# The experts' matmuls of a fused attention and soft-MoE block in three passes over high and low parts

## The reference, cut to what matters

```python
x = layernorm(x) ; se = layernorm(slot_embeds) * scale            # B=4, E=16, S=64, D=256, F=512, DO=256
logits = einsum('bnd,esd->bnes', x, se)
slots = einsum('bnd,bnes->besd', x, softmax(logits, axis=1))
gate = gelu(einsum('besd,edf->besf', slots, Wg) + bg)             # per expert: 256 x 256 by 256 x 512
up = einsum('besd,edf->besf', slots, Wu) + bu                     # the same size
eout = einsum('besf,efo->beso', gate * up, Wd) + bd               # 256 x 512 by 512 x 256
out = x_in + attention(xn) + einsum('bns,bso->bno', combine, eout)
```

## Time and profile before

| | us |
|---|---|
| median of 3 runs (lowest, highest) | 2759.08 (2755.48, 2759.23) |
| the profiled execution's own time | 2755.84 |
| its span, first to last instruction | 2753.9 |
| TensorE busy in the span | 2589.1 (94%) |
| VectorE, ScalarE, GpSimd busy | 2078.8 (75%), 1634.3 (59%), 443.7 (16%) |
| experts' stage, first matmul to first matmul of combine | 2273.5 to 2445.15 |

### The profile page before, as it was taken

One profiled execution on the slowest core, in us unless ns is written; L12 is line 12 of the kernel. 1 busy time (PEld: TensorE's weight loads), 2 busy tenths in 40 slices (PEclk: granted clock), 3 DMA queues, 4 the chain that ended last, 5 costly groups with the idle time before them and its releaser, 6 DMA issues. The chain is left out here.

```text
span 2753.9 us, 47808 instructions
## 1 busy us (share of the span) xinstructions
PE 2589.1 (94%) x16291; PEld 1543.9 (56%) x16291; DVE 2078.8 (75%) x5010; ACT 1634.3 (59%) x3370; POOL 443.7 (16%) x611
## 2 busy tenths in 40 slices
PE   7866999999999999999999999989999999999999
PEld 4433444444444444444444444347878788889999
DVE  8966989899899889989988998738474522346665
ACT  4531777777777777777777777866364522122221
POOL 4533111111111111111111111124121100100000
PEclk9975999999999999999999999999999999999999
DMA  7983362133033123303303000025343345435554
GB/s 244 315 241 40 46 84 34 17 46 45 6 48 45 22 30 46 39 12 46 46 14 40 8 6 8 8 104 214 106 170 136 109 161 180 163 132 194 193 189 156
DMA packets 177641, 257.63 MB, mean 94 GB/s; under 512 B 48756, under 2 KB 126712, under 8 KB 175896
## 3 DMA queue, kind: packets, MB, share of 16 engines
q1 hardware_dynamic: 160824, 239.26, 34.2%
q10 hardware_dynamic: 16608, 15.73, 1.9%
HBM read 158.30 MB, written 95.45 MB: 92 GB/s over the span
## 5 line engine op out<-in xcount | busy, mean ns | idle before, releaser
L768 ACT ACTIVATE att_pr<-att_ring 128x512 f32<-128x512 f32 (+3 forms) x2560 | 1174.4, 548 | 398.7 <-PE att_ring L848 391.4
L815 DVE TENSOR_REDUCE att_mx<-att_ring 128x1 f32<-128x512 f32 x1536 | 968.0, 680 | 77.0 <-PE att_ring L861 73.9
L861 PE MATMUL att_ring<-att_ks,att_qs 48*128 48x512 f32 (+3 forms) x1920 | 647.7, 422 | 17.0 <-ACT att_pr L768 7.0
L848 PE MATMUL att_ring<-att_qs,att_ks 64*128 64x512 f32 (+3 forms) x1920 | 575.0, 406 | 9.8 <-DMA att_qs<-att_mrow 4.9
L848 PEld LDWEIGHTS att_ring<-att_qs,att_ks 64*128 64x128 f32 x1920 | 300.5, 186 | 406.2 <-DVE att_mx L815 143.4
L821 DVE CUSTOM_DVE_ANT_0 att_junk<-att_ring,w_causal 128x256 bf16<-128x256 f32 (+3 forms) x1024 | 466.0, 486 | 67.6 <-PE att_ring L861 42.2
L887 PE MATMUL att_acc<-att_pr,att_v 128*32 128x512 f32 (+3 forms) x3840 | 451.5, 542 | 2.7 <-ACT att_cT L779 1.5
L861 PEld LDWEIGHTS att_ring<-att_ks,att_qs 48*128 48x128 f32 x1920 | 307.4, 185 | 144.7 <-ACT att_pr L768 106.4
L726 POOL TENSOR_SCALAR_AFFINE_SELECT att_pr<-att_pr 128x512 f32<-128x512 f32 x256 | 163.1, 637 | 1049.5 <-ACT att_pr L768 1049.5
L861 PE MATMUL att_ring<-g_ks,g_qs 48*128 48x512 f32 (+3 forms) x640 | 225.5, 463 | 17.2 <-PEq L137 7.8
L1452 ACT CAST com_e1h<-com_tp 128x1024 fp32r<-128x1024 f32 x64 | 64.8, 1017 | 236.4 <-PE com_tp L1512 236.4
(11 more groups left out here) (162 smaller groups left out, 3225.1 us busy)
## 6 DMA issues: line engine op xcount, KB each, us to landing
slot_exps<-dis_e SPq DMA_DIRECT2D x64, 512.0 KB, 2.7
com_e<-slot_exps SPq DMA_DIRECT2D x64, 512.0 KB, 3.5
att_qs<-q_parts SPq DMA_DIRECT2D x72, 256.0 KB, 12.0
q_parts<-proj_part SPq DMA_DIRECT2D x32, 512.0 KB, 4.3
dis_y<-y_rows SPq DMA_DIRECT2D x32, 512.0 KB, 3.9
att_ks<-k_parts SPq DMA_DIRECT2D x72, 128.0 KB, 12.8
y_rows<-proj_y SPq DMA_DIRECT2D x16, 512.0 KB, 4.4
y_cols<-proj_yT SPq DMA_DIRECT2D x16, 512.0 KB, 5.3
```

Source lines behind the costliest of these rows:

```text
L768: nc.scalar.activation(pr[:, s % NPR, h, off:CH], spot(("s", s, h)), ACT.Exp, scale=float(HD) ** -0.5).then_inc(exp_done, 1)
L815: nc.vector.tensor_reduce(dst, spot(e), AX.X, ALU.max).then_inc(mb_used, 1)
L848: nc.tensor.matmul(spot(e), ks[g][r, kb * P:(kb + 1) * P], qs[g][r, c, hf * CH + off:(hf + 1) * CH], start=True, stop=True).then_inc(sT_re ...
L861: nc.tensor.matmul(spot(e), qs[g][r, c, q0:q0 + P], ks[g][r, j * CH:j * CH + wd], start=True, stop=True).then_inc(mb_ready, 1)
```

## The change: what it does

Expert 0's gate and up products stay as they are. For all others, and for all sixteen down products, both operands are held as a high part (rounded to fp32r) and a low part (the difference), and each matmul becomes three: high x high, high x low, low x high. The splits are made beside the matmuls:

- ScalarE makes the high parts of Wg, Wu and Wd (`gate_high`, `up_high`, `down_high`, 128 x 1024 each) and of the four pieces of h (`hidden_high`).
- VectorE makes the low parts of Wu and Wd (`up_low`, `down_low`) and of h (`hidden_low`). Its output step for an expert now comes one expert later: `output(e - 2)` in round e.
- GpSimd makes both parts of the slots (`slots_parts`) and the low part of Wg (`gate_low`), and the low parts of pairs as before.
- The raw weights' rings have two buffers in place of four. `load(e)` waits for the splits of expert e - 2; `load_bias` is as it was, and stands between one `load` and the next.

```diff
-    NB = 4
+    NR, NB = 2, 4
...
-        wg, wu = a.sb("wg", [P, NB, DK, F]), a.sb("wu", [P, NB, DK, F])
-        wd = a.sb("wd", [P, NB, FB, D])
+        wg, wu, wd = a.sb("wg", [P, NR, DK, F]), a.sb("wu", [P, NR, DK, F]), a.sb("wd", [P, NR, FB, D])
...
             def _(sp):
+                def load(e):
+                    if e < E:
+                        for dst, src, loaded, split, n in ((wg, "Wg", gate_in, wg_split, e - NR),
+                                                           (wu, "Wu", up_in, wu_split, e - NR),
+                                                           (wd, "Wd", down_in, wd_split, e - NR + 1)):
+                            if e >= NPRE + NR:
+                                sp.wait_ge(split, n)
+                            sp.dma_start(dst[:, e % NR], io[src][e]).then_inc(loaded[e % NR], 16)
...
                 for e in range(E):
                     if e >= NPRE:
-                        load_gu(e + NB)
-                    if e + NB < E:
-                        load_bias(e + NB)
-                    if e >= NPRE:
-                        load_down(e + NB)
+                        load(e + NR)
+                    load_bias(e + NB)
                     if e == E - NB:
                         com["load_first"](sp)
...
             def _(act):
+                def gate_high(e):
+                    wait_weights(act, e, gate_in)
+                    if e >= 3:
+                        act.wait_ge(gu_ready, 2 * (e - 2) + 2)
+                    nc.scalar.copy(wgh[:, e % 2], weights(e)[0]).then_inc(wg_high, 1)
...
+                gate_high(1)
+                up_high(1)
+                down_high(0)
                 for e in range(E):
-                    for f in range(FB):
...
+                    gelus(e, (0, 1))
+                    if 1 <= e < E - 1:
+                        gate_high(e + 1)
+                    hidden_high(e, (0, 1))
+                    if 1 <= e < E - 1:
+                        up_high(e + 1)
+                    gelus(e, (2, 3))
+                    if e >= 1:
+                        down_high(e)
+                    hidden_high(e, (2, 3))
                     if e >= 3 and e % 2:
                         round_pair((e - 3) // 2)
...
             def _(dve):
+                def up_low(e):
+                    dve.wait_ge(wu_high, e)
+                    nc.vector.tensor_tensor(wul[:, e % 2], weights(e)[1], wuh[:, e % 2].bitcast(F32),
+                                            ALU.subtract).then_inc(wu_split, 1)
...
-                hidden(0)
-                for e in range(1, E):
-                    hidden(e)
-                    output(e - 1)
-                output(E - 1)
+                for e in range(E):
+                    hidden(e, (0, 1))
+                    if e >= 2:
+                        output(e - 2)
+                    hidden_low(e, (0, 1))
+                    if 1 <= e < E - 1:
+                        up_low(e + 1)
+                    hidden(e, (2, 3))
+                    if e >= 1:
+                        down_low(e)
+                    hidden_low(e, (2, 3))
...
             def _(pool):
+                for e in range(1, E):
+                    slots_parts(e)
+                    gate_low(e)
+                    if e >= 5 and e % 2:
+                        pair_low((e - 5) // 2)
...
                 def gate_up(e):
-                        pe.wait_ge(gu_in[q], 16 * 2 * ((e - NPRE) // NB + 1))
+                        pe.wait_ge(sl_split, e)
+                        pe.wait_ge(wg_split, e)
+                        pe.wait_ge(wu_split, e)
...
+                                    for lhs, rhs in ((hi, slh), (hi, sll), (lo, slh)):
+                                        last = nc.tensor.matmul(dst[:, f, :], lhs[:, e % 2, k, cols], rhs[:, e % 2, k, :],
+                                                                start=(k == 0 and rhs is slh and lhs is hi),
+                                                                stop=(k == DK - 1 and lhs is lo))
...
                 def down(e):
+                    pe.wait_ge(wd_split, e + 1)
+                    pe.wait_ge(hl_ready, FB * e + FB)
```

More of the change, by code:

```diff
@@ L1327, in _, with slots_parts, gate_low, pair_low @@
             def _(pool):
-                for s in range(SB - 1):
+                def slots_parts(e):
+                    src = pre["slots"][:, :, e // 2, e % 2]
+                    part = lambda t: t[:, e % 2].rearrange("p k (b j) -> p b k j", b=B)
+                    if e == 1:
+                        pool.wait_ge(pre["slots_in"], 16 * (B - 1))
+                    if e >= 3:
+                        pool.wait_ge(gu_ready, 2 * (e - 2) + 2)
+                    nc.gpsimd.tensor_copy(part(slh), src).then_inc(sl_high, 1)
+                    pool.wait_ge(sl_high, e)
+                    nc.gpsimd.tensor_tensor(part(sll), src, part(slh).bitcast(F32), ALU.subtract).then_inc(sl_split, 1)
+                    pool.wait_ge(sl_split, e)
+                def gate_low(e):
+                    pool.wait_ge(wg_high, e)
+                    nc.gpsimd.tensor_tensor(wgl[:, e % 2], weights(e)[0], wgh[:, e % 2].bitcast(F32),
+                                            ALU.subtract).then_inc(wg_split, 1)
+                    pool.wait_ge(wg_split, e)
+                def pair_low(s):
                     pool.wait_ge(high_ready, s + 1)
@@ L1331, in _ @@
                                             ALU.subtract).then_inc(low_ready, 1)
+                    pool.wait_ge(low_ready, s + 1)
+                for e in range(1, E):
[3 more added lines that the diff above has]
+                        pair_low((e - 5) // 2)
+                pair_low(SB - 2)
             @block.tensor
@@ L1361, in down @@
                     for r in range(RB):
+                        rows = slice(r * P, (r + 1) * P)
                         for f in range(FB):
-                            last = nc.tensor.matmul(op[:, e % 2, r, :], h[:, e % 2, f, r * P:(r + 1) * P],
-                                                    weights(e)[2][:, f, :], start=(f == 0), stop=(f == FB - 1))
+                            for lhs, rhs in ((hh, wdh), (hh, wdl), (hl, wdh)):
+                                last = nc.tensor.matmul(op[:, e % 2, r, :], lhs[:, e % 2, f, rows], rhs[:, e % 2, f, :],
+                                                        start=(f == 0 and lhs is hh and rhs is wdh),
+                                                        stop=(f == FB - 1 and lhs is hl))
                     last.then_inc(o_ready, 1)
```

124 lines of the change are left out of this document (77 added, 47 removed).

## The result

| | before | changed |
|---|---|---|
| median, us (lowest, highest; 4 runs each) | 2758.45 (2755.48, 2759.23) | 2890.3 (2889.12, 2891.83) |
| the profiled execution | 2755.84 | 2889.38 |
| first gelu of the experts' stage | 2278.82 | 2277.85 |
| first matmul of the combine stage | 2445.15 | 2578.39 |

The changed kernel is slower: ratio 1.0486, 95% interval [1.0473, 1.0499]. The forecast was 2856 with a range of 2822 to 2882, so the direction was right and the time lies 8 us above the range. By the profiled executions the change cost 133.5 us, and 133.2 of that stands between the two starts of the combine stage; nothing outside the experts' stage moved.

The account below looks back on a forecast made before the run. TensorE was taken to bound the kernel before; with the change, late weight loads give rounds of 19.8 us. 2304.2 + 217.8 + 9.5 + 9.9 + 4.1 = 2545.5 against 2445.15, so 2755.8 + 100.3 = 2856 us, range 2822 to 2882.

Parts of the forecast that it names:

- The load behind the output step of its own round: Experts 4 to 14: weights requested only after an output step one round before use; Wg issued at 3.69 us.
- The landing, 5.8: Experts' stage: Wg taken to land 5.8 us after issue, at 9.49; 5.2 to 6.2 moves the round -0.6 to +0.4.
- Rival 3: Experts' stage: the load of Wg lands sooner; 5.2 us gives 2849, a skill page's 3.2 us about 2827.
- The clock, 1.8 a round: TensorE's clock falls during over 7 us idle, so the next first half starts slow, adding 1.8 us a round.
- rival 1: VectorE isn't held by GpSimd (2842), or the clock stays up (2836), both 2822; chance 0.20 with a sooner landing.
- VectorE held by GpSimd's low part of Wg: VectorE's low parts of h, ready at 11.0, wait on the shared SBUF port until GpSimd's subtraction ends at 13.0.
- The step that failed: From 13.0, VectorE's two low pieces of h and low part of Wu follow at once, ending at 15.05.
- rival 2: Experts' stage: GpSimd and VectorE take turns at the port, 1 to 2.4 us more a round, 2867 to 2882; chance 0.15.
- the bounds: Stated margins on a round: landing -0.6 to +0.4, clock 0 to +2.2, GpSimd between VectorE's steps up to 2.4 longer.
- Slow for 3.2 us (first case): Clock estimate: TensorE slow for 3.2 us after idling, so the first half takes 4.3 us; slow throughout, 5.0.
- Rival 4: TensorE bounds the experts' stage, weights there in time: rounds of 8.58, 2732 us; chance 0.05, including anything up to the old time.
- Rival 5: The change doesn't do what it says: high and low forms might cost TensorE more than 0.119 us a matmul; slower too.

Follow-up runs that it names:

- e1: Changed kernel with each bias load two experts later in SyncE's list, so weight loads are asked for a round earlier: 2788.38 us, ratio 1.0119.
- e11: Changed kernel with only VectorE's output step moved, ahead of the first two pieces of h: 2849.33 us, ratio 1.0328.
- e3b: Changed kernel with 82 extra unused matmuls per expert after the down product in rounds 3 to 13, filling TensorE's gap: 2873.42 us, ratio 1.0427.
- e2: Changed kernel with GpSimd waiting, after its low part of Wg, for VectorE's low part of Wu: 2865.54 us, ratio 1.0405.
- e9: Changed kernel with a small unused GpSimd subtraction added at the end of the dispatch stage: 2884.07 us, ratio 1.0462.
- e10: e8 with VectorE's low part of Wu behind h's first two pieces, output step last, pair rounding one expert later: 2731.1 us, ratio 0.9897.
- e7: Changed kernel with weight loads and splits an expert earlier, other steps reordered, h in PSUM, waits for two pieces of h: 2755.14 us, ratio 0.9992.
- e8: e7 plus the small GpSimd subtraction of e9 at the end of the dispatch stage: 2750.35 us, ratio 0.9987.

## Why the prediction was right in its course and 33 us short

The chain was right link by link but one. In us from the end of a first half (2356.23 in the round shown):

| link | predicted | round shown | mean of the eleven |
|---|---|---|---|
| output step ends | 3.27 | 3.23 | 3.18 |
| Wg issued | 3.69 | 3.94 | 3.62 |
| copy of Wg starts | 9.54 | 8.89 | 9.20 |
| GpSimd's low part of Wg | 10.65 to 13.0 | 10.08 to 12.43 | 10.38 to 12.73 |
| VectorE's low part of Wu ends | 15.05 | 15.66 | 16.45 |
| TensorE starts | 15.1 | 15.92 | 16.71 |
| its first half, slow at first | 4.7 | 4.7 | 5.04 |
| round | 19.8 | 20.6 | 21.75 |

- **The load behind the output step of its own round: right.** e1 takes it away and 101 us with it; e11 moves it and the round follows.
- **The landing, 5.8: 0.3 to 0.9 too long** (median 5.5, in this round 4.9). Rival 3 was right to that extent; it made the forecast too high, not too low.
- **The clock, 1.8 a round: right in kind, a little small.** The first half took 4.5 to 5.5, and 5.04 in the mean, which is 2.2 more than at full clock. e3b, which kept the clock up in nine of eleven rounds, gained 16 us for the 20 of the sum. The half of rival 1 in which the clock stays up fell.
- **VectorE held by GpSimd's low part of Wg: right,** in every row of the rounds shown. The other half of rival 1 fell too.
- **The step that failed** is the next one: "two pieces of about 0.42 and the low part of Wu at 1.22 end at 15.05". I let VectorE run its three instructions in one go, since they follow each other at once. GpSimd's next subtraction came in between: `exp_wul` took 2.28 in its median, and `exp_hl` x2 4.92 in rounds with a pair. From the end of GpSimd's low part of Wg to that of the low part of Wu I had 2.05; it took 3.23 or so in rounds without a pair, 4.3 in those with one, and 3.72 in the mean. That is rival 2, to which I gave 0.15; the bounds named it (up to 2.4 a round). Its size there was right (1 to 2.4 a round; measured 3.72 - 2.05 = 1.67), and e2 shows it by taking it away (1.75).
- **What no case had:** rival 2 was priced in 11 rounds only. By the profiled executions the 33 us (133.2 less 100.3) are: first gelu 1.0 earlier; to expert 3, 34.05 for 25.4, so 8.7, of which GpSimd's late first subtraction is 4.5 (e9) and turn-taking 4.3 (e2); 11 rounds at 1.95, 21.4; round 14 to 15 13.3 for 9.5, so 3.8. They add up to 32.9. No run has the edits of e2 and e9 alone together, so that their two shares of the 8.7 add up is not shown. Of the 21.4, VectorE's steps are 18.4, the clock 3.7 and TensorE's start 0.26 and not 0.05 behind the low part of Wu 2.3; that GpSimd was done 0.27 earlier takes back 3.0.
- **What could have been counted.** Without the 12.5 at both ends the time would have been in the range. The low parts of slots and pairs there stand in GpSimd's list, and a blank like that of 8.2 us stands in the trace before. The row from which I took the blocking has "7.18 <-issue" on it, and I gave it no price.
- **Slips that change little.** The chances as written add up to 1.01. "Slow for 3.2 us (first case)" is the row of the start of the stage, which stands second. The band for rival 2 went up to 2885, but the range ended at 2882.
- **Rival 4,** TensorE's bound with 2732, was rightly put aside for the kernel as it stands. e10 measured 2731.1 once the loads, GpSimd, h and VectorE's order had all been changed, so its arithmetic (rounds of 8.58, measured 8.48) was sound. **Rival 5** fell: in e10 72 matmuls take 8.48, 0.118 each.

The rule that I had taken from the Trainium skill, "SBUF — State Buffer", section "SBUF: two separate sides", says that the port goes to whoever "starts first" and that the other is blocked for the whole instruction. The rounds above agree with the second half (`exp_wul` 1.06 longer beside `exp_sll`). The rule does not say who comes next when both have work waiting. In these rounds it was GpSimd's instruction, not VectorE's next. But the trace of the kernel before has the other order too: in the dispatch stage VectorE's row of 17 subtractions with two SBUF operands ran on until 2060.22, and GpSimd's copy, 1.04 long at its shortest, took 4.92 and ended 0.9 behind it:

```profile
2049.91 10.31 DVE L1066 TENSOR_TENSOR dis_lg<-dis_lg,dis_cm 128x512 f32<-128x512 f32 x17
...
2056.20 4.92 POOL L1127 CAST dis_yTh<-dis_yTl 128x1024 fp32r<-128x1024 f32 x1 [13.68 <-DMA dis_yTl<-y_cols]
```

So the order isn't always GpSimd's turn, and no run here shows what decides it.

Two more things stay open. With loads early and h in PSUM, e7 and e8 still took rounds over TensorE's 8.5. The two places in VectorE's order and the pair's rounding together mend that, and I did not try them one by one. And what GpSimd does in the 8.2 us isn't shown: the traces name only what stands ahead of them.

## What to carry to other kernels

Before you count instructions, follow each load's releasing wait to the instruction that fulfils it, and ask in which round that runs against the round that uses the data; here the wait of one bias load, at the head of an in-order queue, was worth 100 us. Where VectorE and GpSimd both subtract in SBUF, price every VectorE step also for the case that a waiting GpSimd instruction goes first, or give one operand to PSUM. In a trace that you reason from, give every blank on a row you use a price. And a saving on the busiest engine is only had when every other engine's list fits below the new period in the right order: nearly the same instructions in two orders gave 2750 and 2731.

## What the runs showed of the hardware that I had not expected

- A GpSimd subtraction gets in between two VectorE subtractions that follow each other in VectorE's list: `exp_wul` 2.28 us for the 1.21 of e2, `exp_hl` x2 4.92 for the 2.77 of e2, where nothing gets between.
- A change of GpSimd between a reduction over partitions and a subtraction costs 6.7 to 9.0 us before the subtraction and 5.4 to 6.4 before the reduction, over the traces of all fourteen kernels, and each time a pair of MODIFY_POOL_CONFIG stands ahead of the blank. A small subtraction in the stage ahead takes the blank out of the experts' stage (e9). The Trainium skill, "GPSIMD Engine Reference", section "2.1 Instruction dispatch", tells of "an IRAM-load of approximately 6 µs" at the first call of a kernel that was newly loaded, behind that same instruction. The traces agree with it in the place, and for the reductions in the size; the subtractions take longer.
- In the eleven long gaps of the changed kernel the granted clock fell 3.4 to 4.9 us after TensorE's last matmul had ended, and was full again 3.2 to 6.1 us after the matmuls began again. Shorter gaps went both ways: in e3b nine of 0.7 to 1.8 us left the clock up eight times, and behind one of 1.8 us it fell.
- On an otherwise quiet queue, behind a bias load of 128 KB, 512 KB of weights land in 4.9 us at the shortest and 5.5 in the median.
